# Attention with two softmaxes and mixed experts on one core: all matmuls of a head in tiles of 64 rows by 32 columns, maxima by single banks, ten heads' maxima beside the experts

## The reference, cut to what matters

```python
xn = _layernorm(x, axis=-1)                       # x: 4 x 1024 x 256
x = x + _L0_attn_ref(xn, ...) + _L0_ffn_ref(xn, ...)

# attention: 16 heads of two softmaxes (i = 0, 1), head dimension 8, values 16 wide
def sdpa(qi, ki):
    s = jnp.einsum('bnhd,bmhd->bhnm', qi, ki) * scale
    p = jax.nn.softmax(s, axis=-1)
    return jnp.einsum('bhnm,bmhe->bhne', p, v)
a1 = sdpa(q[:, :, :, 0], k[:, :, :, 0])
a2 = sdpa(q[:, :, :, 1], k[:, :, :, 1])
o = a1 - lam * a2
o = _rms_norm(o, sub_norm_w, EPS) * (1.0 - LAMBDA_INIT)
# then the projection; 64 heads in all (4 batches of 16)

# experts: T = 4096 tokens, top 2 of 8, capacity C = 2T/E = 1024 rows each
h = jax.nn.gelu(jnp.einsum('ecd,edf->ecf', disp, w_gate), approximate=False)
eo = jnp.einsum('ecf,efd->ecd', h, w_down)
```

## Time and profile before

| | |
|---|---|
| Time, median of 3 runs | 1752.79 us (1752.04 to 1753.38) |
| Span of the profiled execution | 1749.3 us |
| Median of the runs less the span | 3.5 us |
| TensorE busy | 97% |
| VectorE busy | 86% |
| ScalarE busy | 80% |
| GpSimd busy | 31% |

### The profile page before, as it was taken

How to read it: one execution, slowest core, us unless ns; L and a number is a source line. 1 busy time by engine, 2 the same in 40 slices (tenths; PEclk the granted TensorE clock), 3 DMA queues, 4 the chain that set the end, 5 groups by cost and what they waited for, 6 DMA issues and landing times.

```text
span 1749.3 us, 38531 instructions
## 1 busy us (share of the span) xinstructions
PE 1697.2 (97%) x15106; PEld 722.6 (41%) x15107; DVE 1503.2 (86%) x1792; ACT 1397.3 (80%) x2637; POOL 537.6 (31%) x1098
## 2 busy tenths in 40 slices
PE   6999999999999999999999999999999999999999
PEld 5557777777773222222222222222222222222227
DVE  7878787787777999999999999999999999999935
ACT  4464534544546999999999999999999999999994
POOL 1124111111000243332433323425534233443344
PEclk9989999999999999999999999999999999999999
DMA  8754333321203111111111111111111111100003
GB/s 261 219 193 137 106 105 103 107 75 54 85 25 115 34 31 41 30 37 36 29 40 32 34 32 35 38 34 33 39 30 36 36 31 39 32 22 14 11 11 103
DMA packets 92276, 109.60 MB, mean 63 GB/s; under 512 B 17472, under 2 KB 67264, under 8 KB 92096
## 3 DMA queue, kind: packets, MB, share of 16 engines
q1 hardware_dynamic: 85952, 90.36, 16.6%
q0 software_dynamic: 6144, 16.79, 3.3%
HBM read 72.77 MB, written 33.82 MB: 61 GB/s over the span
## 4 chain that ended last, share of the span: by engine, by line
PE 67%; ACT 28%; DVE 3%; issue 1%; DMA 1%; ACTq 0%; SPq 0%; DVEq 0%
ACT arena_t L853 25%; PE banks L1326 19%; PE banks L1314 12%; PE banks L1363 10%; PE banks L1296 8%; PE banks L1341 7%; PE banks L1343 4%; PE banks L1406 2%; ACT o_raw L836 2%; PE banks L1199 2%; PE banks L1442 1%; PE banks L1242 1%; DVE rest L951 1%; PE banks L1231 1%; DVE arena_q L958 1%
## 5 line engine op out<-in xcount | busy, mean ns | idle before, releaser
L1066 DVE TENSOR_REDUCE row_half<-banks 128x2 f32<-128x1024 f32 x1024 | 1186.5, 1216 | 81.9 <-PE banks L1296 80.0
L853 ACT ACTIVATE arena_t<-banks 128x512 f32<-128x512 f32 x2048 | 1083.2, 599 | 42.0 <-PE banks L1314 16.5
L1326 PE MATMUL banks<-arena_t,v_ring 128*17 128x256 f32 x8192 | 642.3, 386 | 25.6 <-ACT o_raw L836 25.5
L1326 PEld LDWEIGHTS banks<-arena_t,v_ring 128*17 128x17 f32 x8192 | 136.1, 95 | 408.0 <-issue 240.3
L1314 PE MATMUL banks<-arena_q 50*128 50x512 bf16 x960 | 284.1, 383 | 0.0
L1296 PE MATMUL banks<-arena_q 48*128 48x512 bf16 x960 | 268.5, 384 | 0.2 <-DVE row_half L1066 0.2
L1314 PE MATMUL banks<-qk_ring 50*128 50x512 bf16 x896 | 264.1, 385 | 1.6 <-DVE arena_r L1094 1.5
L1296 PE MATMUL banks<-qk_ring 48*128 48x512 bf16 x896 | 248.6, 382 | 0.0
L818 ACT ACTIVATE arena_t<-banks 128x512 f32<-128x512 f32 x128 | 76.6, 598 | 199.1 <-PE banks L1363 188.0
L1341 PE MATMUL banks<-w_parts,hidden_parts 128*128 128x512 f32 x512 | 186.9, 406 | 1.6 <-DVE arena_r L1094 1.6
L1363 PE MATMUL banks<-rows_parts,w_parts 128*128 128x512 f32 x768 | 183.2, 394 | 2.5 <-DVE rows_parts L1010 2.5
(11 more groups left out here) (150 smaller groups left out, 1488.1 us busy)
## 6 DMA issues: line engine op xcount, KB each, us to landing
expert_rows<-arena_r SPq DMA_DIRECT2D x16, 512.0 KB, 3.2
q_stack<-arena_q SPq DMA_DIRECT2D x8, 768.0 KB, 3.5
k_stack<-arena_q SPq DMA_DIRECT2D x8, 768.0 KB, 4.4
v_ring<-v_heads SPq DMA_DIRECT2D x64, 68.0 KB, 2.9
arena_x<-x_in SPq DMA_DIRECT2D x4, 1024.0 KB, 6.3
token_rows<-arena_x SPq DMA_DIRECT2D x4, 1024.0 KB, 4.8
arena_v<-w_gate_in SPq DMA_DIRECT2D x4, 1024.0 KB, 6.3
arena_v<-w_down_in SPq DMA_DIRECT2D x4, 1024.0 KB, 8.7
```

What stands on the lines that cost most here:

```text
L853: nc.scalar.activation(probs[:, kt % PSLOTS, q, :], banks[:, ST_BANKS[ring_place(i) % 3], :], ACT.Exp).then_inc(exp_done, 1)
L1066: nc.vector.tensor_reduce(halves[:, :, j // 2], banks[:, smax_bank(m):smax_bank(m) + 2, :], AX.X, ALU.max, negate=True).then_inc(smax_done, 1)
L1326: mm = pe.matmul(banks[QUAD * q:QUAD * q + VP, OT_BANK, columns], v_ring[:, g % SLOTS, kt, :], probs[:, kt % PSLOTS, q, columns], start=(k ...
```

## The change

A head's matmuls all get the tile shape 64 rows by 32 columns.

- Scores: a step is 64 keys of both softmaxes for one half of the queries. Four matmuls (2 softmaxes x 2 groups of 32 keys) of 50 rows by 32 columns with 512 queries write one bank: softmax 0 on partitions 0 to 63, softmax 1 on 64 to 127. 32 steps a head, and 32 exponentials of 128 x 512 as before.
- Maxima in the attention: a "half" is 64 queries of both softmaxes and 512 keys, four matmuls into one bank with softmax 1 on partitions 0 to 63 and softmax 0 on 64 to 127, and one reduction 128 x 512 to 128 x 1. Three banks (2, 3, 4). HALVES = 28 of a head's 32 steps have one.
- PV: a group of 64 keys, both softmaxes at once on the two row halves: eight matmuls of 64 rows by 17 columns with 256 queries, into two banks (5 and 6), the accumulator of each softmax in its own; 16 groups a head. The values stand on both row halves of `v_ring`, by two DMAs.
- Beside the experts: ten pairs a chunk instead of eight (the two new ones after gate tile 5), so the first ten heads' maxima are done there; the ring has 12 slots (two more in `rest`).
- The late heads' maxima rows go in by four DMAs instead of eight, and the layout of the negated maxima, the copied output and GpSimd's scaling follow the new order.

```diff
-PSLOTS = 4
-LAG = 2
+PSLOTS = 8
+LAG = 4
-INVERT_AT = 12
-RING = 10
-EARLY = 16 * 8
+INVERT_AT = 24
+RING = 12
+EARLY_HEADS = 10
+EARLY = 2 * 8 * EARLY_HEADS
+KEYS = 64
+KG = N // KEYS
+STEPS = 2 * KG
+HALVES = 28
+BETWEEN = 10
...
-        SMAX_PAIRS = (2, 4)
-        EXPERT_SMAX_PAIRS = (2, 4, 6, 2, 4, 0, 2, 4)
-        OT_BANK = 6
+        HALF_BANKS = (2, 3, 4)
+        EXPERT_SMAX_PAIRS = (2, 4, 6, 2, 4, 2, 4, 0, 2, 4)
+        OT_BANK = 5
...
+        def halves_before(step):
+            return min(LATE_HALVES, step * HALVES // STEPS)
+        def half_at(g, i):
+            step = STEPS * g + i
+            n = halves_before(step)
+            return n if halves_before(step + 1) > n else None
...
             def load_v(g):
-                sp.dma_start(v_ring[:, g % SLOTS].rearrange("p t w -> p (t w)"),
-                             v_heads[g].rearrange("p t w -> p (t w)")).then_inc(v_in[g % SLOTS], 16)
+                for s in range(2):
+                    sp.dma_start(v_ring[KEYS * s:KEYS * (s + 1), g % SLOTS].rearrange("k i t w -> k i (t w)"),
+                                 v_heads[g].rearrange("(i k) t w -> k i (t w)", i=2)).then_inc(v_in[g % SLOTS], 16)
...
+                for i in range(STEPS):
+                    kg, qh = divmod(i, 2)
+                    if qh == 0 and KG * g + kg >= PSLOTS:
+                        act.wait_ge(pv_done, KG * g + kg - PSLOTS + 1)
...
+            def half_max(n):
+                g, u, h = half_of(n)
+                dve.wait_ge(half_psum, n + 1)
+                nc.vector.tensor_reduce(row_half[:, g % 2, h, u:u + 1], banks[:, half_bank(n), :],
+                                        AX.X, ALU.max, negate=True).then_inc(half_done, 1)
...
+                        for m in range(3):
+                            smax(first + m)
+                    if f == 4:
+                        for m in range(3, 5):
+                            smax(first + m)
...
+            def half_scores(n):
+                g, u, h = half_of(n)
+                if n % STEPS == 0:
+                    pe.wait_ge(head_in[g % RING], HEAD_DMAS * 16 * (g // RING + 1))
+                if n >= len(HALF_BANKS):
+                    pe.wait_ge(half_done, n - len(HALF_BANKS) + 1)
+                for c in range(2):
+                    for s in range(2):
+                        rows = slice(HALF * s, HALF * s + STACK)
+                        column = HALF * (1 - s) + QUAD * c
+                        mm = pe.matmul(banks[column:column + QUAD, half_bank(n), :],
+                                       heads_qk[g % RING][rows, 0, KEYS * u + QUAD * c:KEYS * u + QUAD * (c + 1)],
+                                       heads_qk[g % RING][rows, 1, h * CH:(h + 1) * CH], start=True, stop=True)
+                mm.then_inc(half_psum, 1)
...
+                for c in range(2):
+                    for s in range(2):
+                        rows = slice(HALF * s, HALF * s + SROWS)
+                        column = HALF * s + QUAD * c
+                        mm = pe.matmul(banks[column:column + QUAD, ST_BANKS[place % 3], :],
+                                       heads_qk[g % RING][rows, 1, KEYS * kg + QUAD * c:KEYS * kg + QUAD * (c + 1)],
+                                       heads_qk[g % RING][rows, 0, qh * CH:(qh + 1) * CH], start=True, stop=True)
+                mm.then_inc(st_psum, 1)
...
+                for c in range(4):
+                    columns = slice(c % 2 * CH // 2, (c % 2 + 1) * CH // 2)
+                    for s in range(2):
+                        rows = slice(KEYS * s, KEYS * (s + 1))
+                        mm = pe.matmul(banks[QUAD * c:QUAD * c + VP, OT_BANK + s, 0:CH // 2], v_ring[rows, g % SLOTS, kg % 2, kg // 2, :],
+                                       probs[rows, kg % PSLOTS, c // 2, columns], start=(kg == 0), stop=(kg == KG - 1),
+                                       skip_group_check=True)
+                mm.then_inc(pv_done, 1)
...
                 if n + 1 < 2 * E:
-                    pe.wait_ge(smax_done, 8 * n + 3)
+                    pe.wait_ge(smax_done, BETWEEN * n + 6)
                     turn_rows(n + 1)
...
+                for i in range(STEPS):
+                    kg, qh = divmod(i, 2)
+                    if qh == 0:
+                        pv_before(g, kg)
+                        if i == TURN_AT and g > 0:
+                            turn_entry(g)
+                    scores_t(g, kg, qh)
+                    n = half_at(g, i)
+                    if n is not None:
+                        half_scores(n)
```

More of the change, by code:

```diff
@@ L507, in expert_step @@
                     load_down(e + 2, e % 2)
-                if s == 0 and e > 0:
-                    neg_rows_in(e - 1)
+                for h in range(EARLY_HEADS - 1):
+                    if join_chunk(h) == n:
+                        neg_rows_in(h)
             for n in range(2 * E):
@@ L1317, in pv @@
-            def pv(g, kt, half):
-                if half == 0:
-                    if kt == 0:
-                        pe.wait_ge(o_copied, g + 1)
-                        pe.wait_ge(v_in[g % SLOTS], 16 * (g // SLOTS + 1))
-                    pe.wait_ge(exp_done, 32 * g + 4 * kt + 4 + len(ST_BANKS))
-                columns = slice(half * CH // 2, (half + 1) * CH // 2)
-                for q in range(4):
-                    mm = pe.matmul(banks[QUAD * q:QUAD * q + VP, OT_BANK, columns], v_ring[:, g % SLOTS, kt, :],
-                                   probs[:, kt % PSLOTS, q, columns], start=(kt == 0 and half == 0), stop=(kt == TB - 1),
-                                   skip_group_check=True)
-                if half == 1:
-                    mm.then_inc(pv_done, 1)
+                    pe.wait_ge(exp_done, STEPS * g + score_before(place - 3) + 1 + len(ST_BANKS))
@@ L1391, in expert_step @@
                     down_tile(n, f, 2)
-                for j in range(6, 8):
+                for j in range(8, 10):
                     expert_smax(n, j)
```

249 lines of the change are left out of this document (123 added, 126 removed).

## The result

| | before | after |
|---|---|---|
| Median of the runs | 1752.87 us (4 runs) | 1763.49 us (1762.77 to 1764.29, 4 runs) |
| Ratio, 95% interval | | 1.0064 (1.0052 to 1.0077) |
| Span of the profiled execution | 1749.3 us | 1762.4 us |
| Pitch of the heads, from the o_raw copies | 18.27 us | 18.30 us |

The forecast was 1699 us and faster. It was wrong in sign, inside the range.

What follows compares the result with a forecast made beforehand. The prediction took TensorE, slowed by tile shape changes, to set the attention's pitch. With VectorE then binding, -63 us there and +9.5 beside the experts gave -53.5, so 1752.8 to 1699 us; range 1682 to 1775, its own 1684 to 1711.

Steps and rivals of the forecast that it cites:

- Key group without a change of shape: TensorE in the attention: 64 keys of PV, scores and maxima take 0.91 us, against 1.10 now.
- VectorE's work 17.15 us a head: Attention: 28 one-bank reductions of 0.60 us plus some 0.35 us of small operations, making VectorE the bound.
- ScalarE 16.8: Attention: 32 exponentials of 0.50 us, the copy and the taken output, 16.8 us a head at most.
- Rivals 1, 2 and 3: Attention slower: eight tiles not at once (1987 us, 0.08); shared bank excludes (2045, 0.06); TensorE not fed (1924, 0.08).
- rival 2: Attention scores: two row tiles writing one bank exclude each other, a head takes 22.8 us, 2045 us in all; chance 0.06.
- the 0.15 us: Attention: added to VectorE's 17.15 us a head for TensorE's lateness at copied output and turning, giving 17.3.
- The last sentence of the prediction: Attention: the forecast also falls if VectorE idles at each turning, for which three banks are too few.
- The experts: Beside the experts, TensorE-bound: two more pairs a chunk over 16 chunks cost 9.1 to 12.8 us, taken as 9.5.
- The cover for the late low part: Beside the experts: the sixth low part, 1.8 us late, is covered by remaining gate tiles; uncovered up to 29 us.
- Rival 4: Attention: half the gain, eight-tile rounds take 0.25 to 0.27 us, TensorE's head 17.5 to 18.0, 1711 to 1742 us; chance 0.16.
- Rival 5: Attention: no change, the pitch falls by only 0.15 us, what the experts cost; chance 0.04.

Runs made afterwards that it cites:

- e4: Kernel after with values and probabilities in bf16, so each PV matmul is one record instead of two: 1681.8 us, ratio 0.9617 to the kernel before.
- e13: Kernel after without the gather's DMAs in the attention (experts' part of the output missing, GpSimd's arithmetic kept): 1709.8 us, ratio 0.9780 to the kernel before.
- e2: Kernel after with VectorE's attention reductions over 256 of the 512 columns, all matmuls kept: ratio 0.9565 to the kernel before.
- e1: Kernel after with each maxima matmul of 512 columns in the attention split into two of 256: 1760.8 us, ratio 1.0069 to the kernel before.
- e12: Kernel before with only the change beside the experts, ten heads' maxima there, old tile shapes: ratio 1.0043 to the kernel before.
- e9: Kernel after with redundant waits of PV and the turning taken off TensorE, taken over by ScalarE's list: ratio 1.0063 to the kernel before.
- e16: Kernel before without the gather's DMAs: 1748.9 us, ratio 1.0003 to the kernel before.
- e17: Kernel after with the gather of head g issued at step 8 + 5g mod 24: 1740.3 us, ratio 0.9937 to the kernel before.
- e14: Kernel after with each gather issued at step 14 of a head, everything computed: 1710.7 us, ratio 0.9786 to the kernel before.
- e5: Kernel after with the steps without maxima moved from 0, 8, 16, 24 to 4, 12, 20, 28: 1713.75 us, ratio 0.9801 to the kernel before.
- e11: Kernel after with steps without maxima at 4, 12, 20, 28 and redundant waits taken off TensorE: ratio 1.0049 to the kernel before.
- e18: Kernel after with steps without maxima at 4, 12, 20, 28 and gathers at step 14: 1738.5 us, ratio 0.9929 to the kernel before.

## Why the prediction was wrong

**The sizes of the new work were right.** Key group without a change of shape: 0.91 us forecast; the PV group takes 0.43 us and all eight tiles work at once. VectorE's work 17.15 us a head: 17.1 in e4, 945.34 x 18.36 / 1000 = 17.4 in the kernel after, 17.2 in e13. ScalarE 16.8: 16.7 in e2. Rivals 1, 2 and 3 are refuted: the eight tiles start together, a shared bank holds nothing up, and records can come at 12.1 ns (e1). For rival 2 the Trainium skill, page "TensorEngine Tiling (Array Packing)", Gotcha 1, says that row tiles cannot access one PSUM bank simultaneously; the scores of both row tiles of a bank here start together and take no longer (1001.37, four matmuls in 0.40 us), so the measurement decides against the rule's consequence for speed.

**The step that failed is the 0.15 us** "for the two places (copied output, turning) at which TensorE is late". Two things were wrong with it.

First, it allowed for TensorE's own waits only. It left out that something outside the head's list can stop TensorE: the gather, once a head, for 0.3 to 0.9 us. I had written of GpSimd only that it "does the same operations and is 37% busy", and it does. It isn't that the kernel before hid these stalls: it has none. The longest pause between two of its TensorE records from 0.3 to 1.8 us behind a gather is 0.31 us in the mean, as at other places (0.31 to 0.33), both in the trace of the kernel before and in e12, which ran on a chip where e9 has 50 stalls; e16 agrees that its gathers cost nothing. In the kernel after the same measure is 0.47 us, against 0.24 to 0.30 at other places. Measured: in the kernel after's own trace the mean gaps at steps 1, 7 and 9 stand 0.39, 0.16 and 0.22 us above the medians, 0.76 us a head or 49 us in all, and e13 gives 50 us and 0.84 us of pitch. That is more than the stalls' own 0.44 us a head. The likely reason, which no run tests by itself, is that a stall starves VectorE, which has 17.2 us of work in a head of 17.5 and can't make up for it.

Second, the places themselves cost 0.3 us and not 0.15: without any gather the pitch is 17.52, with 17.2 of VectorE's work. (17.52 - 17.3) x 61.7 heads = 14 us. The last sentence of the prediction had named this.

**The experts** cost 12 us and not 9.5: chunks begin 26.49 us apart (median) instead of 25.81, 0.68 x 16 = 11. The cover for the late low part held.

Sum: 1699 + 50 + 14 + 2.5 = 1765.5, measured 1763.5. That the result fell inside the stated range is luck: the range was that wide for rivals 4 and 5, and neither names this cause. Rival 4 foretold 17.5 to 18.0 us of pitch by a slower round; the round isn't slower, and without the stalls (17.52 in e13) its range would have held by another cause. Rival 5, no gain of pitch, came out as to size (18.30), with the experts' cost on top. None of the five had its cause.

**What stays open.** That the stalls come with the gather is shown: they moved with it in e17, are gone without it in e13 (where e14, with its gathers, has none either), and 50 of 50 stand behind it in the kernel after. When a gather stalls TensorE isn't shown. Place alone doesn't decide (e14 against e17), and the kernel after wasn't measured beside the versions that are free of stalls. There it might have taken some 50 us less, an estimate from e13 and e14 (1710 us, with the kernel before at 1748.5); the forecast would then have been right in sign and still 11 to 15 us too low. By what the gather stops TensorE isn't shown either. TensorE goes on 0.2 to 0.6 us behind the end of the gather's record; the Trainium skill, page "Perfetto Trace Analysis", section "DMA Instruction — SWDGE (GPSIMD)", says that this record ends when the last descriptor is written, not when the data has moved. If so, TensorE goes on shortly after the descriptors are there; the trace has the gather's first packets only after that, 1.69 us behind its start or later. No run here shows what the two engines share in that time.

## What to carry to other kernels

Read "issue" pauses in the middle of a group by their distance to events of other engines, move the event, and see whether the pauses move with it (e17); leaving it out (e13) is the second test, not the only one. Setting the means of the steps beside their medians tells sporadic stalls from a worse order, within one trace and on one chip. A stall in a kernel whose fullest engine has 2% to spare can cost more than it lasts: 0.44 us of bare stalls a head stand against 0.76 to 0.84 us of pitch. And before an edit is given the credit, run the unchanged kernel beside it: here that was never done, and versions that differ in little (e5 and e11; e14 and e18), measured on different chips, lie 1.5 to 2.5% apart although each was compared with the kernel before on its own chip. The kernel before doesn't have the stalls, so it can't cancel them out.

## What was unexpected of the hardware

- Behind a GpSimd indirect DMA of 128 rows TensorE can stand still for 0.3 to 0.9 us without waiting for any semaphore, always until 1.26 to 1.67 us behind its start and before the first of its packets moves (1.69 us or more). In other runs, with all engines at the same place to 0.03 us, it doesn't.
- Eight tiles of 64x32 work at once, and TensorE takes records, matmuls and weight loads alike, at 12.1 ns each over 256 of them (e1).
- In e1 TensorE pauses 1.3 to 2.6 us behind instruction packets (69 of 72 pauses); with 500 matmul records a head this is not seen, with 612 it is.
